# State and keys in float16 halves, and low halves, state mask and LayerNorm refinement on GpSimd, in a linear-attention kernel

## The reference

```
x = x + attention(layernorm(x))     # linear attention, 16 heads of 32
    q = relu(..) + 1e-6, k = relu(..) + 1e-6
    kv  = cumsum over rows of k (outer) v      # causal state, 32 x 32 per head
    out = (q . kv) / max(q . cumsum(k), 1e-6)
    attention = out @ out_w.T + out_b
x = x + quantised_linear(layernorm(x))   # int8 input with one scale over all rows, int8 weights
```

## Time and profile before

| | us |
|---|---|
| median of 3 runs | 1270.39 |
| profiled execution, its own time | 1271.68 |
| its span | 1269.9 |
| TensorE matmul busy | 1149.3 (91%) |
| TensorE weight load busy | 849.8 (67%) |
| VectorE busy | 1041.6 (82%) |
| ScalarE busy | 549.7 (43%) |
| GpSimd busy | 700.0 (55%) |
| mean granted TensorE clock | 0.967 of full |

### The profile page before, as it was taken

The page is one execution under the profiler, slowest core; times in us unless marked ns, Lnnn a source line. Parts: engine busy times, 40 slices in busy tenths (PEclk is TensorE's granted clock), DMA queues, the critical chain, the costliest instruction groups (busy, mean ns, idle before and its releaser), DMA issues. The chain is left out here.

```text
span 1269.9 us, 31459 instructions
## 1 busy us (share of the span) xinstructions
PE 1149.3 (91%) x10921; PEld 849.8 (67%) x10931; DVE 1041.6 (82%) x2239; ACT 549.7 (43%) x1130; POOL 700.0 (55%) x847
## 2 busy tenths in 40 slices
PE   4699999999899999999899999998999999974998
PEld 2477777777677767777677767776777777742664
DVE  5668889888789878888788889888888897757887
ACT  4344444444344434444444434443444444422553
POOL 2365556555555555666455555555566665531887
PEclk8899999999899989999899989999999999986999
DMA  5222223222232222322222223223232221240994
GB/s 215 51 60 77 78 77 88 77 78 78 69 80 78 76 83 77 83 84 76 73 76 79 76 70 81 77 77 86 76 84 84 76 84 48 52 144 27 338 339 174
DMA packets 73927, 120.87 MB, mean 95 GB/s; under 512 B 16433, under 2 KB 16945, under 8 KB 73778
## 3 DMA queue, kind: packets, MB, share of 16 engines
q1 hardware_dynamic: 72528, 117.51, 31.2%
q10 hardware_dynamic: 1250, 1.32, 0.4%
HBM read 36.97 MB, written 31.46 MB: 54 GB/s over the span
## 5 line engine op out<-in xcount | busy, mean ns | idle before, releaser
L396 POOL TENSOR_SCALAR_AFFINE_SELECT am_hi<-am_hi 128x512 f16<-128x512 f16 x256 | 173.7, 679 | 373.6 <-DVE am_lo L854 373.6
L446 PE MATMUL unit<-xt_hi,w_hi 128*128 128x256 f16 x1024 | 286.8, 280 | 19.9 <-DVE xt_lo L830 10.9
L446 PE MATMUL unit<-xt_lo,w_hi 128*128 128x256 f16 x1024 | 286.5, 280 | 0.0
L446 PE MATMUL unit<-xt_hi,w_lo 128*128 128x256 f16 x1024 | 286.2, 280 | 0.0
L374 POOL TENSOR_SCALAR q_t<-q_t,eps_scaled 128x256 f32<-128x256 f32 x128 | 118.8, 928 | 133.4 <-ACT q_t L658 133.4
L396 POOL TENSOR_SCALAR_AFFINE_SELECT am_lo<-am_lo 128x512 f16<-128x512 f16 x256 | 177.9, 695 | 0.0
L854 DVE SCALAR_TENSOR_TENSOR am_lo<-sc,am_hi 128x512 f16<-128x512 f32 x256 | 163.4, 678 | 16.8 <-ACT am_hi L685 16.4
L658 ACT ACTIVATE q_t<-unit,qk_bias_scaled 128x256 f32<-128x256 f32 x128 | 60.6, 474 | 227.5 <-PE unit L446 227.5
L685 ACT ACTIVATE am_hi<-sc 128x512 f16<-128x512 f32 x256 | 138.4, 596 | 43.2 <-PE sc L478 43.2
L446 PEld LDWEIGHTS unit<-xt_hi,w_hi 128*128 128x128 f16 x1024 | 102.8, 100 | 46.4 <-DVE xt_lo L830 17.5
L658 ACT ACTIVATE k_t<-unit,qk_bias_scaled 128x256 f32<-128x256 f32 x128 | 60.8, 475 | 132.6 <-PE unit L446 132.6
(11 more groups left out here) (150 smaller groups left out, 2765.1 us busy)
## 6 DMA issues: line engine op xcount, KB each, us to landing
stack<-qk_hi SPq DMA_DIRECT2D x512, 64.0 KB, 2.0
xs<-x SPq DMA_DIRECT2D x64, 256.0 KB, 2.7
stack<-qk_lo SPq DMA_DIRECT2D x256, 64.0 KB, 2.0
out<-res SPq DMA_DIRECT2D x64, 256.0 KB, 3.5
x_spill<-xs SPq DMA_DIRECT2D x56, 256.0 KB, 2.1
x_ring<-x_spill SPq DMA_DIRECT2D x56, 256.0 KB, 4.0
stack<-qkv_wt SPq DMA_DIRECT2D x4, 768.0 KB, 9.4
stack<-out_wt SPq DMA_DIRECT2D x1, 1024.0 KB, 13.2
```

What stands on the lines that cost most here:

```text
L396: ins = pool.affine_select(out=am[:, r, :, :], in_=am[:, r, :, :], compare_op=ALU.is_ge, fill=0.0, base=0, pattern=[[0, HG], [1, CHUNK]], ...
L446: mm = pe.matmul(dst[:, 0:GT], wp[:, k, f:f + P], xp[:, g % 2, k, :], start=(n == 0), stop=(n == len(terms) - 1))
```

## The change

1. `keys_values` and the state part of `outputs` use float16 halves: three float16 matmuls in the place of one float32 one (which the trace counts as two). The state becomes `s_hi`, `s_lo`.
2. Keys are transposed from their float16 halves, eight 128x128 in one PSUM bank of the `unit` pair, as a unit "kt" of their own right behind the transposed x; the copy `kn` is one ScalarE instruction of 128x1024.
3. `add_to_state` adds the whole 128x264 half of `st`; the blocks of other heads are set to zero after that: GpSimd multiplies by `own_head` (`mask_state`), ScalarE writes `s_hi` (`split_state`), GpSimd writes `s_lo`.
4. `split_qk` works on pairs of units (128x512): ScalarE writes `f_t` (float32 with epsilon) and `qk_hi`, GpSimd writes `qk_lo`. The epsilon instructions on GpSimd go. `relu` has four slots.
5. The four small instructions of the LayerNorm refinement move from VectorE to GpSimd (`refine_rstd`).
6. `keys_values` stands ahead of and behind `project_out`, not behind `outputs`; scale factors are changed to fit the number ranges of float16.

```
-            UNITS = [[("xt", 0)] + [("qk", i) for i in range(2, QK)],
-                     [("xt", 1), ("v", 0), ("v", 1), ("qk", 0), ("qk", 1)]]
+            UNITS = [[("xt", 0), ("kt", 0)] + [("qk", i) for i in range(2, QK)],
+                     [("xt", 1), ("kt", 1), ("v", 0), ("v", 1), ("qk", 0), ("qk", 1)]]
...
 # GpSimd
+                def split_qk(b, g, p):
+                    pool.wait_ge(qk_hi_done, upto(b, GROUP * g, PAIRS // GROUP, p + 1))
+                    own = slice(2 * p, 2 * p + 2)
+                    pool.tensor_tensor(qk_lo[:, g % 2, own, :], f_t[:, own, :], qk_hi[:, g % 2, own, :], ALU.subtract
+                                       ).then_inc(qk_lo_done, 1)
+                def mask_state(b, c):
+                    pool.wait_ge(s_added, upto_inner(b, c, 2))
...
+                    pool.tensor_tensor(s_own[:, :, :, :], state[:, :, :, :], own_head[:, :, :, :], ALU.mult).then_inc(s_masked, 1)
+                def split_state(b, c):
+                    pool.wait_ge(s_hi_done, upto_inner(b, c))
+                    pool.tensor_tensor(s_lo[:, :, :, :], s_own[:, :, :, :], s_hi[:, :, :, :], ALU.subtract).then_inc(s_lo_done, 1)
+                def refine_rstd(b, g):
+                    n = b * (CB // GROUP) + g
+                    pool.wait_ge(ln_step, n * LN_STEPS + 1)
+                    pool.tensor_tensor(t0[:, :], r0[:, :], r0[:, :], ALU.mult).then_inc(ln_step, 1)
...
+                    pool.wait_ge(ln_step, n * LN_STEPS + 4)
+                    pool.tensor_tensor(rstd[:, :], r0[:, :], t2[:, :], ALU.mult).then_inc(ln_step, 1)
...
                 def body(b, first, last):
                     for c in range(CB):
+                        g = c // GROUP + 1
+                        more = not (last and g >= CB // GROUP)
                         for r in range(4):
+                            if r == 2:
+                                if c > 0:
+                                    split_state(b, c - 1)
+                                if more:
+                                    split_qk(b, g, 3 if c % GROUP == 1 else 0)
...
+                        if more and c % GROUP == 0:
+                            split_qk(b, g, 1)
+                        if c % GROUP == 1 and not (last and g + 2 >= CB // GROUP):
+                            refine_rstd(b, g + 2)
                         if not (last and c >= CB - AHEAD):
                             add_bias(b, c + AHEAD)
+                        if c < CB - 1:
+                            mask_state(b, c)
...
 # TensorE, outputs
-                            pe.matmul(o[:, half, i * 4 * VW:(i + 1) * 4 * VW], q_t[:, par, g, at],
-                                      state[:, g, :, :].rearrange("p h w -> p (h w)"),
+                            for qp, sp_ in ((qk_hi, s_hi), (qk_hi, s_lo), (qk_lo, s_hi)):
+                                pe.matmul(o[:, half, i * 4 * VW:(i + 1) * 4 * VW], qp[:, par, HG + g, at],
+                                          sp_[:, g, :, :].rearrange("p h w -> p (h w)"),
...
 # TensorE, body
                         if not (first and c == 0):
                             transpose_attn(b, c - 1)
+                        if c < CB - 1:
+                            transpose_keys(b, c)
                         projections(2 if c % GROUP == 0 else 1)
...
+                        if c < CB - 1:
+                            keys_values(b, c, 0, first)
                         if not (first and c == 0):
                             project_out(b, c - 1)
+                        if c < CB - 1:
+                            keys_values(b, c, 1, first)
                         projections(1)
-                        if c < CB - 1:
-                            transpose_keys(b, c, first)
                         outputs(b, c, 0, first)
                         if c % GROUP == 0:
                             projections(1)
                         outputs(b, c, 1, first)
-                        if c < CB - 1:
-                            keys_values(b, c, 0, first)
                         projections(len(todo))
-                        if c < CB - 1:
-                            keys_values(b, c, 1, first)
...
 # ScalarE
+                def split_qk(b, g, p):
+                    at, own = slice(2 * p % 4, 2 * p % 4 + 2), slice(2 * p, 2 * p + 2)
...
+                    act.activation(f_t[:, own, :], relu[:, at, :], ACT.Identity, bias=eps_scaled[:, side:side + 1]).then_inc(qk_eps_done, 1)
+                    act.activation(qk_hi[:, g % 2, own, :], relu[:, at, :], ACT.Identity, bias=eps_scaled[:, side:side + 1]
+                                   ).then_inc(qk_hi_done, 1)
...
 # VectorE
                     dve.reciprocal(r0[:, :], sq[:, :]).then_inc(ln_step, 1)
-                    dve.wait_ge(ln_step, n * LN_STEPS + 1)
-                    dve.tensor_tensor(t0[:, :], r0[:, :], r0[:, :], ALU.mult).then_inc(ln_step, 1)
...
-                    dve.wait_ge(ln_step, n * LN_STEPS + 4)
-                    dve.tensor_tensor(rstd[:, :], r0[:, :], t2[:, :], ALU.mult).then_inc(ln_step, 1)
                     dve.wait_ge(ln_step, n * LN_STEPS + 5)
...
-                    for r in range(4):
-                        own = state[D * r:D * (r + 1), 2 * half:2 * half + 2, r, :]
...
-                            ins = dve.tensor_tensor(own, new, own, ALU.add)
-                    ins.then_inc(s_updated, 1)
+                    own = state[:, 2 * half:2 * half + 2, :, :].rearrange("p g h w -> p (g h w)")
+                    new = st[:, 0:8 * VW]
...
+                        ins = dve.scalar_tensor_tensor(out=own, in0=new, scalar=SCORE_FACTOR, in1=own, op0=ALU.mult, op1=ALU.add)
+                    ins.then_inc(s_added, 1)
```

More of the change, by code:

```diff
@@ L276, in projections_of @@
             def projections_of(c, last):
-                units = [(c // GROUP + (2 if u in UNITS[1] and u[0] == "qk" else 1), u) for u in UNITS[c % GROUP][1:]]
+                units = [(c // GROUP + (2 if u in UNITS[1] and u[0] == "qk" else 1), u) for u in UNITS[c % GROUP][2:]]
                 return [(g, u) for g, u in units if not (last and g >= CB // GROUP)]
@@ L435, in transpose_x, with transpose_keys @@
                     mm.then_inc(xt_ready, 1)
+                def transpose_keys(b, c):
+                    par, at = place(c)
+                    if isinstance(b, int) and b * CB + c == 0:
+                        pe.wait_ge(ident_half_ready, 1)
+                        pe.wait_ge(qk_lo_done, PAIRS // 2)
+                    dst = take_bank(b, "kt", c, 0).bitcast(F16)
+                    for p, part in enumerate((qk_hi, qk_lo)):
+                        for g in range(HG):
+                            mm = pe.transpose(dst[:, (p * HG + g) * P:(p * HG + g + 1) * P], part[:, par, g, at], ident_half[:, :])
+                    mm.then_inc(kt_ready, 1)
                 def project_qk(b, g, i):
@@ L484, in transpose_attn @@
                     pe.wait_ge(attn_ready, upto(b, c))
-                    if c % CB < CB - 1:
-                        pe.wait_ge(kn_copied, upto_inner(b, c))
+                    if not (isinstance(b, int) and b * CB + c == 0):
+                        pe.wait_ge(x1_ready, upto(b, c - 1))
                     for i in range(EC):
@@ L499, in project_out @@
                     mm.then_inc(op_ready, 1)
-                def transpose_keys(b, c, first):
-                    par, at = place(c)
-                    if not (first and c == 0):
-                        pe.wait_ge(x1_ready, upto(b, c - 1))
-                    for g in range(HG):
-                        mm = pe.transpose(misc[:, g * P:(g + 1) * P], k_t[:, par, g, at], ident[:, :])
-                    mm.then_inc(kn_ready, 1)
                 def outputs(b, c, half, first):
@@ L720, in _ @@
                 ln_root(0, 1)
-                for i in range(2, QK):
-                    features(0, 0, i)
-                    if i < 6:
-                        split_qk(0, 0, (i - 2,))
-                split_qk(0, 0, range(4, QK))
+                for p in range(1, PAIRS):
+                    features(0, 0, 2 * p)
+                    features(0, 0, 2 * p + 1)
+                    split_qk(0, 0, p - 1)
+                split_qk(0, 0, PAIRS - 1)
                 for c in range(GROUP, AHEAD):
```

215 lines of the change are left out of this document (116 added, 99 removed).

## The result

The changed kernel takes 1295.9 us (median of 4 runs, 1294.3 to 1298.5) against 1270.9 us: slower by a ratio of 1.0199 (95% interval 1.0182 to 1.0216). Its profiled execution took 1296.1 us with a span of 1294.3, 24.4 more than the span before (1269.9). The text before forecast 1318, in a range of 1252 to 1362. The direction, the mechanism and the places are as forecast; the size is not: 47 us of loss were forecast and 25 measured, because two terms were too large.

The account below looks back on a forecast made before the run. TensorE bounds phase one, with VectorE right behind. The profiled 1271.7 us plus 31 for the longer batches and 17 for slow clock gives 1320, or 1318 as a median; range 1252 to 1362.

Parts of the forecast that it names:

- The time: Whole kernel: slower, 1318 us as a median against 1270.9, from the loop's added time and slow clock.
- TensorE's own work: Phase one: float16 products at 0.056 us per 132-column matmul cut TensorE's work from 31.8 to 30.5 us a group.
- Odd chunk: Odd chunks: `xt_lo` comes late, first v unit starts at +3.2 after 1.4 us idle; 16.65 us in all.
- The refinement: LayerNorm in odd chunks: four two-column operations on GpSimd take 1.0 us, bounds 0.4 to 3.7.
- `xn` held up, one by the bias, one by the masked state: Odd chunk's end: VectorE's two `xn` wait for GpSimd's instructions, the second ends at +17.4, where denominators then start.
- Rival (1): `xn` isn't held up by GpSimd: even chunk 16.5, group 33.2, kernel 1259 us; chance 20%.
- Even chunk: Even chunks: output transposed at +2.1, qk 2 started at +4.8, masks just in time; 18.3 us in all.
- A batch +3.95 us: Loop: summed chunks make a batch 141.85 us against 137.9, +31 us in all with the shorter last batch.
- 18.5 (chunk 0, with the slow clock described next): First chunk of a batch, after the turn: 18.5 us of the batch's 141.85.
- Clock: Even chunks: idle TensorE drops to 1.2 GHz in 5 of 24, 3.4 us each, 17 us; bounds 0 and 82.
- Start of phase one: Before the loop: fewer VectorE and more GpSimd instructions, taken as no change, +-5 us.

Follow-up runs that it names:

- the run of 1218.5 us: Changed kernel, GpSimd resting during both `xn`, ScalarE's third half pair behind `xt_hi`, x1 maximum/minimum behind `split_attn`, GpSimd's pair-0 low half behind later masks: 0.9571 of before.
- 1248.1: Changed kernel plus one wait: after the refinement GpSimd issues nothing until both `xn` of VectorE are done; 1248.1 us, 0.9807 of before.
- 1266.5: Changed kernel with GpSimd's wait for the `xn` placed behind the bias sum, so only the bias runs beside them; 1266.5 us, 0.9952 of before.
- 1231.4: Changed kernel with GpSimd resting during both `xn`, and ScalarE's third half pair moved from even chunk's end to behind odd chunk's `xt_hi`; 1231.4 us, 0.9691 of before.

## Why the prediction was right, step by step

*The time: in the range, and the size was off.* 1295.9 us lies 1 us above the lower end of what the text called the forecast's own range (1295 to 1350), so landing in that one was partly luck. The sum over the loop was 30 us too high, and 6 us that it had left out made the miss smaller. What bears the forecast out are the rows below, not the total.

*TensorE's own work: right.* The 132-column float16 matmuls follow at 0.055 to 0.06 us and the eight key transposes take 0.46. With most waits out of the way the change does make the group shorter: the run of 1218.5 us shows 16.15 + 15.93 at best against 33.9.

*Odd chunk: right.* Forecast a v unit at +3.2 with 1.4 idle and 16.65 in all; measured +3.16, 1.22 by the profile's idle time (1.4 by distances between starts, as the forecast counted) and 16.61. Taking the halves from in front of `xt_hi` ended this wait and made the chunk 0.46 us shorter; the rest went to the state addition. The bank order was the wrong place for a remedy.

*The refinement: right in size.* Four small operations of 0.19 to 0.20 us, about 0.28 from start to start and once 0.35: 1.1 us, forecast 1.0 between 0.4 and 3.7.

*`xn` held up, one by the bias, one by the masked state: right, and shown by three runs* (1248.1, 1266.5, 1295.9 us for none, one and both). The denominators were forecast at +17.4 and stand at 519.99 - 502.83 = +17.2. By the Trainium skill's page SBUF — State Buffer, "SBUF: two separate sides", this is the exclusive lock of the shared port pair, held for a whole instruction. The trace agrees in what it shows: every held `xn` ends 0.28 us after an instruction of GpSimd. That is less than the 0.54 of one alone, so a part of it passes while it is held. Rival (1), `xn` free, was 1259 us; the run that made it free gave 1248.1. Its group of 33.2 us was right (33.3 measured), its gain over before was half of the measured one: it had left the batch turn as it was, like the forecast.

*Even chunk: right.* Forecast `attn` transposed at +2.1, qk 2 at +4.8, 18.3 in all; measured +1.92, +4.49, 18.31.

*A batch +3.95 us: too large, by the turn.* The term that was mis-sized is "18.5 (chunk 0, with the slow clock described next)". Chunk 0 takes 15.2 us in most batches, since the clock falls at only one of the turns between batches, and 18.5 less the 3.4 us that the forecast took for a fall is 15.1. With the last chunk of the batch before (18.2 to 18.7, forecast 18.47) the turn takes some 33.7 us where the forecast had 37.0 and the kernel before 36.2. The windows there (us, then busy time of each engine, the granted clock third from the end) answer to the earlier trace rows:

```profile
485.00:487.00 2.00, 0.24 (x3) 0.00 (x0) 1.86 (x5) 0.47 (x1) 1.63 (x2) 1.00 0.00 0
487.00:489.00 2.00, 1.41 (x17) 1.40 (x18) 1.85 (x5) 0.71 (x2) 0.00 (x0) 1.00 0.03 8
```

TensorE idles here as before, and the clock stays at 2.4 GHz. Why it fell before at this place and does not now, no run settles; in the run of 1248.1 us it is low again at four turns, for 3.5 us each. From the first denominators to the last the loop takes 1082.5 us against 1064.5, +18.0, where I had 31 + 17 = 48.

*Clock: the place right, the size wrong.* I took 5 falls in even chunks at 3.4 us each, the price of a turn's fall in the kernel before. Six even chunks have one, and it starts 4.2 to 4.8 us into the chunk, around the end of TensorE's idle time there. But the clock stays low for 3.5 us each time, where four of the five turns before had 6.8 to 6.9, and such a chunk takes some 19.66 us in place of 18.31: 1.35 each and 8 in all. One of them, in the same columns:

```profile
664.00:668.00 4.00, 3.66 (x19) 2.58 (x20) 2.08 (x4) 2.18 (x4) 2.98 (x5) 0.57 0.21 66
```

The two errors have one origin: both prices were taken from the turn of the kernel before, as if it would stay as it was.

*Start of phase one: taken as 0 +-5, measured +5.9* (the first denominators end at 83.2 against 77.3). Some 3.2 of it belong to that one execution: TensorE's first transposition starts at 12.8, against 9.1 before, and of two experiments with the same code up to there (1248.1 and 1231.4 us) one starts at 9.4 and the other at 13.0. In the one that starts at 9.4 the first denominators end at 80.0, so about 2.7 us are the change's.

Together 5.9 + 18.0 + 0.5 behind the loop are the 24.4 us of span.

## What to carry to other kernels

Before moving work from VectorE to GpSimd, look at what VectorE runs at that moment rather than at the busy shares. A long two-input GpSimd operation beside VectorE operations that it does not hold up costs VectorE nothing; next to a short SBUF-to-SBUF operation on the critical chain the same one cost 0.9 us, most of its own 1.3 to 1.5. Order is the remedy and it is cheap: one wait on GpSimd that lets VectorE's two short instructions go first was worth 48 us here. And a freed wait should be followed to the next one before it is priced: of four reorderings, two (the bank order, and the maximum and minimum behind `xt_lo`) lost 12 to 13 us against the run that they were added to, because another engine had been just in time.

## What the runs showed of the hardware

- Which VectorE operations are held up beside a two-input GpSimd operation: two-column float32 products and scalings, 0.9 to 1.3 us (0.16 alone), a float32 128x512 scaling, 1.40 to 1.53 (0.54), the copy of 128x32 statistics, 1.30 (0.18). Which are not, with the same duration beside it and alone: the statistics (0.68), the maximum (0.69), and those that read a PSUM bank (`attn` 0.69, `xt_lo` 0.68 to 0.69, the state addition 0.42).
- They end with GpSimd's instruction: small ones 0.01 to 0.03 us after it, `xn` 0.28 after. The other side pays too: the masked state takes 1.49 beside `xn` and 1.31 when GpSimd had waited.
- A two-column operation on GpSimd takes 0.19 us, and 0.28 from start to start where each needs the one before; VectorE's takes 0.16 alone.
- Two executions of kernels with the same beginning differ by 3.6 us in TensorE's first transposition; a start of a few us is not to be read from one profile.
